# Products that follow W1's blocks as they land, stagings inside the product blocks, kernel products of four heads, and four thresholds compared on ScalarE

## The reference

```python
# layer 0: per head a long convolution, masked by a length per batch
K = 2.0 * einsum('hn,hnl->hl', Cs, exp(dtA[:, :, None] * arange(L))).real    # H x L, N = 64 states
y = irfft(rfft(u * mask, 2L) * rfft(K, 2L))[..., :L] + (u * mask) * D         # then masked again
# layer 1: x W1^T plus a gated low-rank term (8 experts of rank 16, top 2 by logit + language bias)
# layer 2: x W2^T plus a low-rank term chosen by a label (5 x rank 32)
# layer 3: x w_eff^T, with W3 quantised by a codebook of 64 values
lora_delta = lora_B @ lora_A * 0.5
normalized = (weight + lora_delta).reshape(O, 8, 128) / exp(scale_log)
idx = searchsorted((cb[:-1] + cb[1:]) * 0.5, normalized)                      # cb: codebook / max|codebook|
w_eff = (cb[idx] - normalized + normalized) * scale + lora_delta
```

## Time and profile before

| | us |
|---|---|
| median of 3 runs | 1037.75 (1037.08 to 1039.02) |
| the profiled execution's own time | 1038.91 |
| its span | 1037.1 |
| TensorE busy | 1001.4 (97%) |
| VectorE busy | 846.2 (82%) |
| ScalarE busy | 428.3 (41%) |
| GpSimd busy | 274.8 (26%) |
| mean granted clock | 0.995 |

### The profile page before, as it was taken

The page is one execution under the profiler, slowest core; times in us unless marked ns, Lnnn a source line. Parts: engine busy times, 40 slices in busy tenths (PEclk is TensorE's granted clock), DMA queues, the critical chain, the costliest instruction groups (busy, mean ns, idle before and its releaser), DMA issues.

```text
span 1037.1 us, 16623 instructions
## 1 busy us (share of the span) xinstructions
PE 1001.4 (97%) x4855; PEld 799.4 (77%) x4855; DVE 846.2 (82%) x1684; ACT 428.3 (41%) x847; POOL 274.8 (26%) x310
## 2 busy tenths in 40 slices
PE   2999999999999999999999999999999999999996
PEld 1555555988888778888888888888888888888885
DVE  5888888999987488888888888888888888888861
ACT  3211313222275445444454435453454445443531
POOL 2200100273455332223322232223222332223100
PEclk9999999999999999999999999999999999999999
DMA  8701010010202344545444554445454544445311
GB/s 257 169 21 61 21 40 1 1 41 1 41 0 42 62 82 74 91 77 103 83 84 78 101 92 76 86 82 103 78 89 74 104 87 80 82 91 99 57 37 41
DMA packets 316659, 74.97 MB, mean 72 GB/s; under 512 B 292490, under 2 KB 309194, under 8 KB 316626
## 3 DMA queue, kind: packets, MB, share of 16 engines
q1 hardware_dynamic: 316626, 74.56, 36.9%
HBM read 57.61 MB, written 16.91 MB: 72 GB/s over the span
## 4 chain that ended last, share of the span: by engine, by line
PE 92%; DVE 2%; ACT 2%; DMA 1%; issue 1%; SPq 0%; DVEq 0%; ACTq 0%
PE bank L633 33%; PE bank L809 13%; PE bank L760 12%; PE bank L623 10%; PE bank L654 4%; PE bank L603 4%; PE bank L592 4%; PE bank L614 3%; PE bank L660 2%; PE bank L768 2%; PE bank L644 1%; PE bank L719 1%; PE bank L581 1%; PE bank L776 1%; PE bank L714 1%
## 5 line engine op out<-in xcount | busy, mean ns | idle before, releaser
L633 PE MATMUL bank<-Mh,strips_r 128*128 128x512 f32 x1024 | 289.9, 395 | 0.0
L633 PEld LDWEIGHTS bank<-Mh,strips_r 128*128 128x128 f32 x1024 | 190.7, 188 | 41.5
L883 ACT ACTIVATE SK<-ZZ 64x448 f32<-64x448 f32 x128 | 73.9, 577 | 211.4 <-DVE ZZ L1168 209.0
L633 PE MATMUL bank<-Ml,strips_r 128*128 128x512 f32 x512 | 160.6, 395 | 0.0
L475 POOL TENSOR_TENSOR Cl<-QC,Ch 128x256 fp32r<-128x256 f32 x32 | 37.2, 1161 | 454.1 <-ACT Ch L865 454.1
L1168 DVE SCALAR_TENSOR_TENSOR ZZ<-ZZ,coef 128x192 f32<-128x192 f32 (+1 forms) x256 | 120.3, 509 | 10.1 <-DVE ZZ L1159 0.3
L760 PE MATMUL bank<-E,A 128*128 128x512 f32 (+1 forms) x384 | 126.1, 489 | 0.0
L633 PEld LDWEIGHTS bank<-Ml,strips_r 128*128 128x128 f32 x512 | 96.2, 188 | 22.6
L760 PEld LDWEIGHTS bank<-E,A 128*128 128x128 f32 x384 | 63.9, 192 | 61.8 <-issue 61.8
L623 PE MATMUL bank<-Mh,strips_r 128*128 128x296 f32 x512 | 110.4, 299 | 0.3 <-DVE strips_r L1187 0.3
L623 PEld LDWEIGHTS bank<-Mh,strips_r 128*128 128x128 f32 x512 | 85.1, 189 | 5.4 <-issue 5.2
(11 more groups left out here) (277 smaller groups left out, 1687.7 us busy)
## 6 DMA issues: line engine op xcount, KB each, us to landing
X<-in_x SPq DMA_DIRECT2D x256, 64.0 KB, 2.6
XT<-in_x SPq DMA_DIRECT2D x256, 64.0 KB, 2.5
out_x<-O SPq DMA_DIRECT2D x64, 256.0 KB, 3.2
toep<-kpad SPq DMA_DIRECT2D x128, 64.0 KB, 2.1
E<-in_L_cond_W SPq DMA_DIRECT2D x8, 512.0 KB, 7.5
W2s<-in_L_cond_W SPq DMA_DIRECT2D x8, 512.0 KB, 4.3
vq<-in_L_cond_weight SPq DMA_DIRECT2D x8, 512.0 KB, 3.4
LA<-in_L_cond_lora_A SPq DMA_DIRECT2D x8, 80.0 KB, 3.4
```

What stands on the lines that cost most here:

```text
L633: pe.matmul(psO[nh][:, :], xs[:, c, :], ms[:, c, nh * BANK:(nh + 1) * BANK], start=(c == 0 and n == 0), stop=False)
L883: act.activation(SK[ri * N:(ri + 1) * N, hh, :].rearrange("p (c b) -> p c b", b=B), ZZ[hh * N:(hh + 1) * N, :, ri, :], ACT.Copy).then_inc( ...
```

## The change

- SP loads the codebook, the scale's logarithms (now as 8 rows of 4 KB, transposed on TensorE by a new job `scale`), then W1's blocks, each with a semaphore of its own, then W2 block 1 and the rest; W2 block 0 and nine small DMAs are issued by ScalarE's queue ahead of its first copy.
- GpSimd adds the diagonal to each W1 block when it has landed. Between the blocks it does the first exponential and the angles of `nat` in steps of 64 x 65 or 64 x 64, which VectorE did before.
- `qt` 0 (without its last 128 columns) becomes `qt0`, whose products go block by block of W1, for two banks. The other `qt` are in four parts: columns 0 to 511 over half of the blocks, the other half, columns 512 to 1023, columns 1024 to 1151. Stagings stand between the parts.
- ScalarE compares 4 thresholds of each quarter (`compare`, with Sign, into bytes `over`); VectorE adds each with one instruction of 2048 columns and runs its own pair for the other 5.
- The rest of `nat` on VectorE comes after quarter 0.
- `kern` makes 16 products of a 128 x 128 stationary (4 heads x 32 rows) and 16 moving columns (4 heads x 4), of which ScalarE takes the diagonal blocks in 4 copies. They stand 4 each ahead of the first four products of `m` (3, 6).

```diff
-        order = [("b3t", 0), ("b3t", 1), ("codesT",)] + deltas(0) + [("w2t", 0, 0), ("w2t", 0, 1)]
-        between = {0: [("codes",)], 1: [("nat4",), ("at", 0), ("at", 1), ("wrt",)], 2: deltas(1), 5: deltas(2), NC - 1: deltas(3)}
+        order = [("w2t", 0, 0), ("w2t", 0, 1), ("scale",), ("qt0", 0), ("codesT",), ("qt0", 1), ("codes",), ("w2t", 1, 0), ("w2t", 1, 1)]
+        order += [("qt", 1, 0), ("b3t", 0), ("b3t", 1), ("qt", 1, 1)] + deltas(0) + [("w2t", 2, 0), ("w2t", 2, 1), ("qt", 1, 2)]
...
+        order += deltas(3)[:2]
+        for mt in range(MT):
+            order += [("lap", mt)] + ([("a3", 0, mt)] if mt < 4 else [])
+        order += deltas(3)[2:]
...
-                pool.wait_ge(ld_w1, 16 * NC)
-                for it in range(NC):
+                def e1_diagonal(it):
+                    pool.wait_ge(ld_w1[it], 16)
                     d = E1[:, it, it * P:(it + 1) * P]
                     pool.tensor_tensor(d, d, ident[:, :], ALU.add).then_inc(e1_ready, 1)
...
+                def qt0(part):
+                    if part == 0:
+                        pe.wait_ge(a2_ready, 1)
+                        pe.wait_ge(stage_free, jobno[("w2t", 0, 1)] + 1)
+                    for it in range(part * NC // 2, (part + 1) * NC // 2):
+                        pe.wait_ge(e1_ready, it + 1)
+                        for n in range(2):
+                            last = pe.matmul(bank[2 + n][:, :], A2[:, it, 0:P], E1[:, it, n * BANK:(n + 1) * BANK],
+                                             start=(it == 0), stop=(it == NC - 1))
...
-                    for h in range(H):
-                        last = pe.matmul(bank[2][0:SPAN, PARTS * h:PARTS * (h + 1)], Vt[:, h, :], X1T[:, h, 0:PARTS], start=True, stop=True)
+                    for g in range(part * H // 16, (part + 1) * H // 16):
+                        heads = slice(4 * g, 4 * g + 4)
+                        last = pe.matmul(bank[2][:, 16 * g:16 * (g + 1)].rearrange("p (h k) -> p h k", k=PARTS),
+                                         Vt[:, heads, :].rearrange("p h r -> p (h r)"), X1T[:, heads, 0:PARTS], start=True, stop=True)
...
+                act.dma_start(W2s[:, 0, :], W2[0:P, :]).then_inc(ld_w2[0], 16)
+                act.dma_start(logs[:, 0:1], log_dt.rearrange("(h a) -> h a", a=1)).then_inc(ld_kgen, 16)
...
+                def compare(q, n):
+                    act.wait_ge(v_ready, q + 1)
+                    act.activation(over[q // 2][:, n, :], vq[:, :, :].rearrange("p t k -> p (t k)"), ACT.Sign,
+                                   bias=fixed_tau[:, n:n + 1]).then_inc(above_done, 1)
...
+                        if (q, n) == (0, 0):
+                            act.wait_ge(quant_done, 2)
...
+                        if q == 0 and 4 <= mt < 4 + FIXED:
+                            compare(3, mt - 4)
...
+                    for n in range(FIXED):
+                        dve.wait_ge(above_done, FIXED * q + n + 1)
+                        step(dve.scalar_tensor_tensor(qf, over[q // 2][:, n, :], fixed_rise[:, n:n + 1], qf, ALU.mult, ALU.add))
```

More of the change, by code:

```diff
@@ L180, in resid_stack_kernel @@
     sel = place("sel", [K_CODES, K_CODES], F32)
+    cursor[0] = max(cursor[0], region_carry + 4 * 5 * EW)
+    nat = place("nat", [H, 16, N], F32)
+    logs = place("logs", [H, 1 + N], F32)
+    exps = place("exps", [H, 1 + N], F32)
+    c_in = place("c_in", [H, N, 2], F32)
+    nat4 = place("nat4", [H, 4, 2 * N], F32)
+    ex = place("ex", [P, 6, H], F32)
+    ex_bits = place("ex_bits", [P, H], I32)
+    nx = place("nx", [H, 7, 1 + N], F32)
+    nx_bits = place("nx_bits", [H, 1 + N], I32)
     assert cursor[0] <= region_carry + 4 * NC * EW
@@ L267, in resid_stack_kernel @@
                 order += [("m", q, mt)]
-                if q + 1 < QUARTERS and mt in (2, 4, 6, 8):
-                    order += [("a3", q + 1, mt // 2 - 1)]
-        jobs = [j for j in order if j[0] not in ("qt", "m")]
+                if q + 1 < QUARTERS and mt in (3, 5, 7, 8):
+                    order += [("a3", q + 1, (3, 5, 7, 8).index(mt))]
+        jobs = [j for j in order if j[0] not in ("b3t", "qt0", "qt", "m")]
         jobno = {j: n for n, j in enumerate(jobs)}
@@ new lines, in poly @@
+                def poly(n):
+                    step(pool.tensor_scalar(t[5], t[5], 1.0 / math.factorial(n), None, ALU.add))
+                    step(pool.tensor_tensor(t[5], t[5], t[4], ALU.mult))
+                e1_diagonal(0)
+                a2_diagonal(0)
+                e1_diagonal(1)
+                pool.wait_ge(e1_ready, 2)
+                pool.wait_ge(a2_ready, 1)
+                pool.wait_ge(ld_kgen, 48)
+                step(pool.tensor_scalar(t[0], logs[:, :], -87.0, 88.0, ALU.max, ALU.min))
@@ new lines, in _ @@
+                poly(6)
+                e1_diagonal(4)
+                pool.wait_ge(e1_ready, 5)
+                poly(5)
+                poly(4)
+                e1_diagonal(5)
+                pool.wait_ge(e1_ready, 6)
+                poly(3)
+                poly(2)
+                e1_diagonal(6)
+                pool.wait_ge(e1_ready, 7)
+                poly(1)
+                step(pool.tensor_scalar(t[5], t[5], 1.0, None, ALU.add))
+                e1_diagonal(7)
+                pool.wait_ge(e1_ready, 8)
@@ L808, in m @@
                         lhs = Bw3[:, kt, :] if mt == MT else QT[:, kt, mt * P:(mt + 1) * P]
+                        if (q, mt) == (LAST_Q, KERN_IN) and kt < 4:
+                            kern(kt)
                         last = pe.matmul(m_bank(n)[0:rows, 0:QO], lhs, A3[q % 2][:, kt, :], start=(kt == 0), stop=(kt == NC - 1))
                     last.then_inc(m_full, 1)
-                do = dict(b3t=b3t, delta=delta, w2t=w2t, codesT=codes_t, codes=codes, nat4=nat4_t, at=at, wrt=wrt, qt=qt, lap=lap,
+                do = dict(scale=scale_t, b3t=b3t, delta=delta, w2t=w2t, codesT=codes_t, codes=codes, nat4=nat4_t, at=at, wrt=wrt, qt0=qt0, qt=qt, lap=lap,
                           a3=a3, m=m)
@@ L821, in _ @@
                             chunk_states(0, hh, first=True)
-                        kern()
                     elif j == ("m", LAST_Q, 6):
@@ L1030, in _ @@
                         take(j, AT[:, :, ER:ER + E], stage(j)[:, 0:NC * E].rearrange("p (c e) -> p c e", c=NC))
-                    elif name == "qt":
-                        kt = which[0]
+                        compare(0, 0)
+                        compare(0, 1)
+                    elif name == "qt0" or (name == "qt" and which[1] == 2):
+                        kt = 0 if name == "qt0" else which[0]
+                        if j == ("qt0", 0):
+                            continue
                         if kt == 2:
@@ L1047, in _ @@
                         take(j, LAp[:, mt, :], stage(j)[:, 0:LR])
+                        if 4 <= mt < 4 + FIXED:
+                            compare(2, mt - 4)
                         if mt == MT - 1:
```

402 lines of the change are left out of this document (240 added, 162 removed).

## The result

The changed kernel takes 1022.1 us (median of 4 executions, 1021.9 to 1023.7) against 1038.4 us (1037.1 to 1042.1): a ratio of 0.985, with a 95% interval of 0.982 to 0.987. Predicted were 1020.5 us and a range of 1009 to 1030. Its profiled execution took 1022.2 us, of which the span is 1020.4.

The account below looks back on a forecast made before the run. TensorE's products were taken to bound the kernel almost everywhere. Gains of 15.2 us up to `m` and 2.5 in it, 17.7 off the profiled 1038.9, gave 1021.2; it said 1020.5, range 1009 to 1030.

Parts of the forecast that it names:

- The first product: First product of `qt` 0 on TensorE: at 9.5 us instead of 28.75, a gain of 19.2 us.
- W1's landing: W1's load at the start: the last block lands near 15 us, while TensorE reaches it at about 24.
- The clock behind the first product: TensorE's low clock in the first products of `qt0`: costs 3.0 us, bounds 0 and 5.
- GpSimd: 0.42 a step: GpSimd's small steps between diagonals at the start: 0.42 us each, hidden with 2 us to spare.
- Rival 1: GpSimd's steps at the start take 0.7 us each and TensorE waits about 7: 1028 us; chance 0.12.
- Stagings: TensorE's idleness at stagings before `m` falls from 5.4 to 3.9 us; gain 1.5, plus 1.7 from the clock.
- the dip at 64.7: Clock of 0.57 at `nat4`, `at`, `wrt` and a W2 block in a row: gone once they stand apart, 1.7 us.
- Rival 5: Stagings don't help: idleness and clock dips stay and `qt0` runs low throughout, 1028 us; chance 0.05.
- the 4.2 us of moved work: b3t, delta, one W2 block and codesT, moved from before the first product to behind it: 4.2 us given back.
- the margin at `m` (1, 0): TensorE's need at `m` (1, 0) for ScalarE's last `a3` copy, ready at 217, needed at 218.5: met by 1 us.
- Rivals 2 and 4: VectorE some us late to quarter 3: 1026 us, chance 0.12; byte-operand passes take 4.6 us, twice: 1048 us, chance 0.04.
- The kernel products: Around `m` (3, 6): products take 3.4 us, gaining 0.7, and the half-clock block behind goes, 1.8; gain 2.5.

Follow-up runs that it names:

- w2first: The changed kernel with W2's block 0 first in SyncE's queue and only three issues ahead of ScalarE's first copy: 1021.8 us, ratio 0.984.

## Why the prediction was right

**The first product: too early by 1.3 us.** The term was 9.5, measured is 10.81. The order of steps was right; the mis-sized one is ScalarE's queue: 7.1 us for ten issues (0.7 each, one of 1.49) where nine by 0.5 and one by 1.27 were taken from SP's queue. The gain is 17.9, not 19.2. W2 block 0 first in SyncE's queue, with three issues on ScalarE, brings the first product to 9.61 and confirms the step. The experiment with all of W1 first shows that 8.4 us of it hang on the separate semaphores. The rest goes with W1's earlier load and with b3t, delta and a W2 block moved behind; it wasn't divided further.

**W1's landing: 18 in place of 15**, still well ahead of the product that needs the last block (24). The rate of 389 GB/s was taken from 3 us on; the trace has 70 GB/s up to 5 us, 361 from 5 to 10 and 393 from 10 to 15. SP's issue of A3raw at 8.63 took 7.16 us; no engine waited for it.

**The clock behind the first product: 2.7 for 3.0**, from 9.6 us against 6.9 for equal halves. In size right; the six other traces that have both halves of `qt0` without idle products or W2's block first lost 1.8 to 3.0. The reading that it rests on is a little off: the kernel before wasn't at 1.2 GHz up to 28.7. The first eight weight loads of the 16 transposes took 1.57 us and the next four, from 27.46, 0.48, so the full clock was there at about 27.5.

**GpSimd: 0.42 a step, 0.45 measured.** The chain ends at 28.7 instead of 26: 0.9 by the later start, the rest by steps and diagonals a little longer. A2's second diagonal was hidden by 1.0 us, not 2. Rival 1 is out; w2first shows how thin the cover is, since its wait at 29 becomes 1.2 us. (The prediction's 36 for 0.7 a step is 35.2 by its own terms.)

**Stagings: 3.9 us idle forecast, 3.73 measured** (155.25 - 151.52), so of the term's two halves the 1.5 for idleness stands (1.7). The other, 1.7 for the dip at 64.7, came true in number and not by its reason. The changed kernel has no dip there, but neither have the two other traces in which `nat4`, `at`, `wrt` and a W2 block still stand in a row (the kernel before with its kernel products alone, narrow and wide). The dip belonged to that one execution of the kernel before, and no run shows that the new places of the stagings took it away. Rival 5 is out.

**`m` starts at 183.8 for 182.2**: 1.0 of it by the end of `qt0` (27.7 for 26.7). The other 0.6 has no row of its own; the 4.2 us of moved work were halves and estimates.

**VectorE: right in every step that is shown.** A pass with a byte operand takes 2.38 us (2.29 taken), quarter 0 takes 47.7 (41.57 to 89.24), the same as forecast, and quarter 3 is normalised at 207.5 for 205, from a start 2.6 later. ScalarE waits 5.1 us for it (5 forecast), and the margin at `m` (1, 0) was 1.3 us where 1 was forecast. Rivals 2 and 4 are out, and the run with nine compares on VectorE shows what they guard against.

**The kernel products: sum right, one reason wrong.** 16 products took 3.24 us (3.4 forecast, 4.1 before), and the stretch gained 2.4 (2.5 forecast). But "with full products between the small ones I count this as gone" isn't borne out: of nine traces with that order four have the dip, and the two with the products in a row have it both. The changed kernel's two traces happen to be among the five. What the runs show in its place is a dip that comes in some executions and not in others (with the products spread out, only in the second batch), and a Toeplitz table that takes 0.7 to 0.9 us of the loss back where it comes. That the term's sum was right is in so far luck: where the dip comes it is 1.7 to 3.4 too high before the table gives its part back.

The rule that a weight load costs by its columns (the Trainium skill, TensorE: Matmul & The Clock Gate, "LDWEIGHTS (loading the stationary operand)") gives 107 ns for 128 columns, and a record took 0.10 us: the trace agrees. By it nothing would have been gained in the products; the trace has 0.9 us less, since 32 columns had cost 32 ns and not 27, and 128 cost 101.

**Sum.** 13.6 up to `m` (15.2 forecast) and 2.8 in it (2.5 forecast; 0.54 us of it is the wait for GpSimd's additions ahead of `m` (3, 0), at 306.99 in the kernel before, that had no term): 16.4, against 17.7. By its own step from the profiled execution to the median (1.2 from 1021.2) the forecast would have been 1020.0; it says 1020.5. Some 3.5 of the 17.7 (1.7 at 64.7 and 1.8 behind the kernel products) were put on two dips of the one profiled execution before. For neither is the forecast's reason shown, so that much of the agreement is luck; without them the sum would be near 1024, still in the range.

## What to carry to other kernels

- A first product that waits for a whole matrix is worth splitting by blocks with a semaphore each, and the DMA issues ahead of a chain's first step belong in its sum, each with its own queue's price.
- When TensorE comes earlier, look for the engine that feeds it last: here 11 of 16 us would have gone back without relief for VectorE, though VectorE didn't bound anything before.
- A dip of the clock in one trace isn't a fixed cost: look at it in several executions of the same kernel, in one batch, before a gain is put down to an edit, and ask what waits behind it, since that can hide the dip and its cure alike. The dip at 64.7 was read as the fault of the order of the work, and two other traces with the same order don't have it.

## What the runs showed of the hardware

- A DMA issue on ScalarE took 0.41 to 1.49 us; eight 512 KB issues on SP took 5.65 us, and one of 256 KB, the third behind them, 7.16.
- Between 128-column weight loads 64 moving float32 columns cost as much as 16: 0.10 us a record.
- Behind products of 16 moving columns the clock fell to 0.50 for 3 to 7 us in 5 of 10 traces, four of them of one batch; behind those of 64 columns in none of 3, all of another batch. Behind `nat4`, `at`, `wrt` and a W2 block in a row it fell in one of 3 traces with the same waits.
- In most of the kernels the slower executions are those with the lower mean clock: w2first took 1023.5 us at 0.996 and 1020.5 at 0.999. What decides in one execution whether a dip comes stays open.
- Behind 12 idle products the full clock was there within 5.5 us of their start, and it was lost again behind 1.77 us of idleness and while the 8-column transposes ran, for about 7 us (10.0 to 16.9).
- Two 128x128 additions on GpSimd took 2.19 us in the changed kernel and 3.49 at the same place with nine compares on VectorE, and TensorE waited for them.
